# A graph-attention kernel whose GpSimd waits, before each batch of gathers, for the landing of the last gather of the batch ahead

## The reference

```
xw = (x @ W).reshape(N, H, CPH)
a_s = einsum('nhc,hc->nh', xw, att_src);  a_d = einsum('nhc,hc->nh', xw, att_dst)
e = leaky_relu(a_s[src] + a_d[dst], 0.2)
m = segment_max(e, dst);  p = exp(e - m[dst]);  s = segment_sum(p, dst)
out = segment_sum(xw[src] * (p / s[dst])[:, :, None], dst)
```

## Time and profile before

| | us |
|---|---|
| median of 3 runs | 3142.78 |
| lowest and highest run | 3138.01 and 3143.33 |
| span of the profiled execution | 3949.4 |
| busy: POOL, DVE, PE, ACT | 1927.4, 2043.1, 1918.5, 1578.9 |
| first and last start of a batch's gather (L882) | 285.3 and 2789.5 |

### The profile page before, as it was taken

How to read it: one execution, slowest core, us unless ns; L and a number is a source line. 1 busy time by engine, 2 the same in 40 slices (tenths; PEclk the granted TensorE clock), 3 DMA queues, 4 the chain that set the end, 5 groups by cost and what they waited for, 6 DMA issues and landing times.

```text
span 3949.4 us, 38354 instructions
## 1 busy us (share of the span) xinstructions
PE 1918.5 (49%) x10116; PEld 1741.9 (44%) x10117; DVE 2043.1 (52%) x4266; ACT 1578.9 (40%) x2552; POOL 1927.4 (49%) x1920
## 2 busy tenths in 40 slices
PE   4500000134435354453544454545213489999998
PEld 2400000123425344353544453435213389999998
DVE  5465676625527355363554563545687544444443
ACT  4322223315536355453555554445323323333332
POOL 4467657645554555535555555465466612222222
PEclk8755555556767676676677776766655599999999
DMA  8244449313332333323333333233365622222222
GB/s 299 76 117 135 144 161 155 120 42 94 94 94 86 94 93 92 94 80 96 94 96 92 94 92 93 59 99 93 119 220 179 230 42 37 36 36 37 36 36 32
DMA packets 212942, 396.68 MB, mean 100 GB/s; under 512 B 76396, under 2 KB 164785, under 8 KB 206305
## 3 DMA queue, kind: packets, MB, share of 16 engines
q1 hardware_dynamic: 136049, 245.72, 18.4%
q0 software_dynamic: 75664, 149.21, 16.8%
q10 hardware_dynamic: 1120, 0.52, 0.0%
HBM read 203.53 MB, written 191.78 MB: 100 GB/s over the span
## 4 chain that ended last, share of the span: by engine, by line
PE 34%; issue 25%; DVE 16%; DVEq 10%; another core or an unknown queue 8%; ACT 4%; SPq 1%; POOL 1%; DMA 1%; POOLq 0%; ACTq 0%
PE ps L1299 13%; PE ps L1390 9%; PE ps L1396 9%; DVEq L1703 5%; DVE AR L1708 4%; PE ps L1270 1%; ACT onehot L1155 1%; ACT AR L1084 1%; DVEq L1709 1%; DVE AR L1773 1%; POOL AR L882 1%; DVE group_stats L1945 1%; ACT onehot L1159 1%; PE ps L1381 1%
## 5 line engine op out<-in xcount | busy, mean ns | idle before, releaser
L882 POOL DMA_INDIRECT AR<-tables,idx x1443 | 1377.0, 954 | 1095.5 <-DMA state<-AR 620.8
L1299 PE MATMUL ps<-table_parts,onehot 128*128 128x408 f32 (+1 forms) x4080 | 953.7, 388 | 1218.1 <-issue 752.5
L1299 PEld LDWEIGHTS ps<-table_parts,onehot 128*128 128x128 f32 x4080 | 861.9, 221 | 1309.9 <-issue 949.7
L1771 DVE TENSOR_SCALAR AR<-ps,tile_pick 128x136 f32<-128x136 f32 x120 | 35.4, 351 | 991.2 <-PE ps L1299 555.4
L1084 ACT COPY AR<-AR 128x1984 f32<-128x1984 f32 (+3 forms) x110 | 392.0, 3564 | 355.1 <-DVE AR L1708 195.6
L956 POOL DMA_INDIRECT out<-AR,idb x105 | 183.5, 1748 | 597.6 <-issue 560.1
L1708 DVE TENSOR_TENSOR_SCAN AR<-ps,AR 128x512 f32<-128x512 f32 x404 | 454.2, 1197 | 0.0
L1390 PEld LDWEIGHTS ps<-AR 128*128 128x128 f32 x3360 | 393.9, 193 | 6.6 <-DVE AR L2164 1.3
L1390 PE MATMUL ps<-AR 128*128 128x128 f32 x3360 | 394.5, 276 | 0.9 <-DVE AR L2164 0.9
L1701 DVE TENSOR_TENSOR AR<-AR,ps 128x3968 f32<-128x3968 f32 (+1 forms) x51 | 356.7, 6994 | 20.7 <-ACT AR L1103 13.4
L1101 ACT ACTIVATE ps<-AR 128x248 f32<-128x248 f32 (+1 forms) x51 | 19.2, 376 | 702.4 <-DVE AR L1688 411.4
(11 more groups left out here) (345 smaller groups left out, 2352.4 us busy)
## 6 DMA issues: line engine op xcount, KB each, us to landing
state<-AR SPq DMA_DIRECT2D x50, 2232.0 KB
AR<-tables,idx POOLq DMA_INDIRECT x1492
AR<-in_L_ffn_W SPq DMA_DIRECT2D x16, 1024.0 KB
AR<-placed SPq DMA_DIRECT2D x105, 130.0 KB, 2.0
adstart<-room SPq DMA_DIRECT2D x26, 496.0 KB
AR<-adstart SPq DMA_DIRECT2D x50, 248.0 KB
tables<-AR SPq DMA_DIRECT2D x49, 136.0 KB
room<-tables SPq DMA_DIRECT2D x14, 476.0 KB
```

Source lines behind the costliest of these rows:

```text
L882: pool.indirect_dma_start(out=G[s][:, j, 0:ROWT], out_offset=None, in_=table_rows, in_offset=bass.IndirectOffsetOnAxis(ap=idx[:, s, j:j + ...
L1299: return T.matmul(bank[:, 0:z], mark, table_parts[:, k, v * w:v * w + z], start=(a == 0 and k == 0), stop=(a == LEV - 1 and k == PARTS - 1))
```

## The change

Before the first gather of each batch but the first, POOL waits until the semaphore of the preceding batch's buffer has the count that tells that all gathers of that batch have landed. It is the same semaphore and count for which DVE waits before it works on that batch.

```diff
@@ -878,6 +878,8 @@
                 s = slot(b)
                 pool.wait_ge(idx_loaded[s], idx_count(b))
                 pool.wait_ge(batch_stored[s], free_count(b))
+                if b >= 1:
+                    pool.wait_ge(batch_gathered[slot(b - 1)], gather_count(b - 1))
                 for j in range(fetched_columns(b)):
                     pool.indirect_dma_start(out=G[s][:, j, 0:ROWT], out_offset=None, in_=table_rows,
                                             in_offset=bass.IndirectOffsetOnAxis(ap=idx[:, s, j:j + 1], axis=0)).then_inc(batch_gathered[s], 16)
```

## The result

The change makes the kernel slower by 260.8 us, where 187 were forecast:

| | before | after |
|---|---|---|
| median of the runs, us | 3143.06 | 3403.89 |
| lowest and highest run | 3138.01 and 3144.07 | 3401.66 and 3408.25 |
| ratio to before, with its 95% interval | | 1.0839 [1.0825, 1.0852] |
| span of the profiled execution | 3949.4 | 3399.9 |

What follows compares the result with a forecast made beforehand. The prediction took the unprofiled kernel to be bound by the issue of gathers on GpSimd. Early boundaries 19 us plus late ones 168 us, batch 50 nothing, made 187 us, so 3330 us, range 3225 to 3395 us.

Steps and rivals of the forecast that it cites:

- The holes as the profiler's: Idle time put down to "issue" in DVE's and PE's rows belongs to the profiled execution alone, 806.6 us over the median.
- The bound, 35.0 us per late batch: On POOL, issuing gathers at 1.25 us each bounds the unprofiled run; a batch of 28 takes 35.0 us.
- The 55 us: Measured 3142.78 us lies 55 us below the gather floor; holes in the stages ahead and behind, or a 1.21 us pace.
- the gather floor: 1430 gathers of batches 0 to 49 at 1.25 us, with the stages ahead and behind: 3198 us.
- The plain boundary, 2.1 us: Between batches without other traffic: 1.25 us landing plus 1.15 restart less 0.30 ordinary gap; nine early ones cost 19 us.
- The first rival: Gathers slip between the store's pieces, so each of 49 boundaries costs 2.1 us: 103 us, 3246 us; chance 0.25.
- A landing held to the store's end: In batches 10 to 49 the last gathers, issued into the store, land with its end: 40 x (39.2 - 35.0) = 168 us.
- the late round: Landing to landing in batches 10 to 49: 0.5 us restart, 30.4 to the store's issue, 8.3 to its end, 39.2 us.
- the 8.3 us: Time from a late store's issue to its DMA's end, taken between two profile readings, 8.6 and 7.9 us.
- The third rival: Late batches cost more: pace 1.21 us and the store's end give 3374 us, DVE's restart of 1.15 us 3400; chance 0.07.
- Batch 50 and the end: Batch 50's 13 gathers land after 18.4 us, covered by DVE's 29.3 us: 0; 2 us if that cover went.
- The second rival: At the boundaries GpSimd's slack hides the wait if the pace is under 0.97 us: no cost, 3143 us; chance 0.10.

Runs made afterwards that it cites:

- all but eight: The change with POOL waiting only for all but the last eight gathers of the preceding batch, DVE for all: 3141.27 us, 1.0004 to the kernel before.
- the later store: The change, with SP issuing the store of batches 9 to 49 only when the next batch's gathers have landed: 3274.45 us, 1.0428 to the kernel before.
- the control without the wait: The kernel before, without the change's wait, with the store of batches 9 to 49 put off until the next batch's gathers have landed: 3139.67 us, 1.0000.

## Why the prediction fell short, step by step

With the trace of all but eight as a stand-in for before, the 260.6 us between the two spans (3399.9 and 3139.3) split at DVE's starts of batches 0, 9 and 49. First the stand-in, then the change:

```profile
281.23 0.57 DVE L1689 TENSOR_TENSOR AR<-AR,ps 128x248 f32<-128x248 f32 x1 [9.72 <-DMA AR<-tables,idx]
644.65 0.59 DVE L1689 TENSOR_TENSOR AR<-AR,ps 128x248 f32<-128x248 f32 x1 [9.67 <-DMA AR<-tables,idx]
2050.57 0.57 DVE L1689 TENSOR_TENSOR AR<-AR,ps 128x248 f32<-128x248 f32 x1 [7.96 <-DMA AR<-tables,idx]
```

```profile
281.90 0.57 DVE L1682 TENSOR_TENSOR AR<-AR,ps 128x248 f32<-128x248 f32 x1 [10.13 <-DMA AR<-tables,idx]
681.81 0.59 DVE L1682 TENSOR_TENSOR AR<-AR,ps 128x248 f32<-128x248 f32 x1 [11.84 <-DMA AR<-tables,idx]
2305.13 0.57 DVE L1682 TENSOR_TENSOR AR<-AR,ps 128x248 f32<-128x248 f32 x1 [11.27 <-DMA AR<-tables,idx]
```

| stretch | all but eight | the change | more | forecast |
|---|---|---|---|---|
| to batch 0 | 281.2 | 281.9 | 0.7 | 0 |
| batch 0 to 9 | 363.4 | 399.9 | 36.5 | 19 |
| batch 9 to 49 | 1405.9 | 1623.3 | 217.4 | 168 |
| batch 49 to the end | 1088.7 | 1094.8 | 6.1 | 0 |

**The holes as the profiler's: right.** The profiles of the change and of all the experiments have spans within 4.2 us of their medians, among them three of kernels as fast as before or faster in which POOL waits 2.4 to 7.2 us in all, ahead of its batch gathers, for anything but its issue. What made the holes in the one profile of before no run shows. One row that the prediction leans on is misread: in batch 5 POOL did gather, from 565.98 us on, when DVE's step came after 0.64 us. So the two rows show a step with a hole and one without, and nothing of what POOL has to do with it.

**The bound, 35.0 us per late batch: right.** 35.0 us from first gather to first gather, 35.15 us per batch at DVE; and fewer gathers shorten the kernel before by 1.23 us each. The 55 us by which the gather floor lay too high were holes, too: up to DVE's start of batch 0 the profile of before takes 326.8 us and the clean trace 281.2, from batch 49's start to the end 1123.5 and 1088.7.

**The plain boundary, 2.1 us: right in size**, 2.0 to 2.4 us with the store put off. But the early boundaries are not all plain: 36.5 us over nine, where 19 were forecast. One of them, ahead of batch 7, costs 14.2 us by its own run. Two more are long in the trace of the change, those ahead of batches 1 and 6:

```profile
282.65 0.94 POOL L884 DMA_INDIRECT AR<-tables,idx  x1 [6.81 <-DMA AR<-tables,idx]
...
497.62 0.97 POOL L884 DMA_INDIRECT AR<-tables,idx  x1 [4.23 <-DMA AR<-tables,idx]
```

The other six have 1.1 to 2.6 us of idle time, as forecast. So the term was taken as 9 equal boundaries from one row, with no look at what else SP issues between batches 1 and 9. The 4.23 us come with SP's load of the table, 3332 KB, which L703 issues at 490.45 us, 1.6 us ahead of the end of batch 5's last gather, the 6.81 us with a row of loads of parameters (L673 to L676) that SP issues from 274.25 us on; no run moved either.

**A landing held to the store's end: right as to the time**, and it carried most of the loss. The first rival's price (2.1 us each, 3246 us) falls by the measured time, by the run with the later store and by that with one gather less. What holds the landing is less plain. In the prediction a rule of the Trainium skill (DMA: Bandwidth & Descriptors, section Queues, rings and completion order), turns by packets of some 9 to 17 descriptors, was read as speaking for less than the whole store. One put-off store, in the window 758.7 to 764.4 us, moves 128 packets, 8 for each of the 16 engines, and no gather's packet moves beside them, though POOL goes on issuing gathers from 758.64 us:

```profile
q1 hardware_dynamic: 128, 2.29, 102.4%
```

If a packet of the trace is a descriptor in the Trainium skill's words, an estimate by its figure of 9 to 17 is one turn for the whole store, and this trace agrees. The change's own trace doesn't. There the store (q1) has the engines to itself only at first; in the window 758.4 to 761.6 us the gathers' packets (q0) move between the store's:

```profile
q1 hardware_dynamic: 66, 0.91, 66.6%
q0 software_dynamic: 110, 0.25, 20.0%
```

So gathers do slip in between the store's pieces there, as the first rival said, and yet the last of the four that wait, issued from 752.96 us on, has its last bytes at 762.0 us, 0.4 us after the store's. Whether the engines' turns or the three gathers ahead of it on its own queue make it so late, no run tells: why the landing comes just with the store's end stays open. The same section of the Trainium skill says that a DMA's semaphore counts only after the earlier writes of that engine, whichever queue they came from, which foresees the same; no run here tests that by itself, and it isn't needed for the put-off store, since there the gathers' bytes themselves come late.

**The step that failed is the size of the late round, 39.2 us forecast and 40.58 measured.** Averages over batches 10 to 46, read from the trace's records: from L1682 to the store 30.4 us, as forecast; from the store's issue to its last byte 9.2 us and not 8.3; from the last byte to L1682 1.1 us and not 0.5, for which no row was at hand, only two bounds. The two rows behind the 8.3 us were not to blame: over the same batches the stores in the trace of before take 8.5 us on average. But those in the trace of all but eight, a kernel as fast as before, take 9.2 us, as in the change. So most of the 0.9 us is missing because the store was read from the one profile with the holes. The sum is 40.7; the last round, from batch 48 to 49, is 37.0 us, which makes 40.58 on average over all 40. These 1.4 us on 40 rounds make 55 us; the base's 35.15 instead of 35.0 takes 6 back; together the 49 us by which the late term was short. Of the 74 us that the forecast lacks, these are 49, the early boundaries 17.5, and the two ends 7. The third rival was nearest in its time, 3374 to 3400 us, and right in a longer restart, but came to it by a pace of 1.21 us that the profile doesn't show (35.0 / 28 = 1.25).

**Batch 50 and the end: 0 forecast, 6 us in the table.** From batch 49's start to batch 50's both kernels take 22.4 us, so the cover held; the 6 us come behind it, and no experiment looked there.

**The second rival** (no cost, decided at a pace under 0.97 us) falls with the measured pace.

**What was said of the profile after:** no first gather of batches 1 to 50 has 0.30 us of idle time, but several have 1.1 us and not 2; late ones follow the quiet end of the store, as said. That the profiled execution might lengthen by less was beside the point: without the holes it is 549.5 us shorter.

## What to carry to other kernels

A wait on the last of a row of transfers costs the round trip of that one, and that is the landing beside whatever is moving at that time, not the quiet landing of the profile: here the 1.6 us from the last gather's end to DVE's start became 3.7 to 6.5, because the store of the batch ahead falls on the last gathers. Waiting for all but the last four of the same row cost 4.6 us, for all but the last eight nothing. When a landing joins a loop, add up the whole loop (here DVE, ACT, SP, store, landing) from averages over many batches, in a trace whose span agrees with the runs; half a microsecond in each of 40 rounds is 20 us.

## What the runs showed of the hardware that was not expected

- The store of the codes in batch 6 kept the DMA engines' queues busy (share 1.68) for 12.5 us at 27 GB/s, and gathers issued beside it landed up to 14.7 us after their start, while a store of 2232 KB took 6.4 us at 402 GB/s. In those 12.5 us the trace has 7119 packets with 0.13 MB on its queue, some 18 bytes each.
- A store behind three small loads on SP's queue moves its first byte 2.4 us after its issue; issued some 7 us after them (the later store) 0.8 us after, and it is over after 6.9 us instead of 9.2 (averages over batches 10 to 46). In the control without the wait, where POOL goes on gathering, it is 0.9 us, too. A part of the change's price may so be that of the loads ahead of the store; that was not tried by itself.
